# Second cross attention: two heads in a 32-row lane, weights divided on GpSimd, keys as 128 + 26

## What is computed

```python
def proj(x, W, bias):
    return (x @ W.T + bias).reshape(b, -1, NH, DK).transpose(0, 2, 1, 3)   # NH = 16, DK = 16
q, k, v = proj(X, Wq, bq), proj(ctx, Wk, bk), proj(ctx, Wv, bv)
scores = jnp.einsum('bhqd,bhkd->bhqk', q, k) / jnp.sqrt(jnp.float32(DK))
scores = jnp.where(attn_mask[:, None, :, :], jnp.float32(-1000000000.0), scores)
attn = jax.nn.softmax(scores, axis=-1)
ctx = jnp.einsum('bhqk,bhkd->bhqd', attn, v)
x = x + ctx.transpose(0, 2, 1, 3).reshape(b, -1, NH * DK) @ Wo.T + bo
```

## Time and profile before

| | |
|---|---|
| median of 3 executions | 2185.2 us (2185.1 to 2185.9) |
| the profiled execution | 2184.0 us, span of its instructions 2182.1 us |
| busy in the span | PE 1971.4, DVE 1548.9, ACT 1235.0, POOL 917.2 us |
| mean granted clock of PE | 0.949 of full |
| stage E | from about 1500 us to 1734 us of the span |

### The profile page before, as it was taken

The page is one execution under the profiler, slowest core; times in us unless marked ns, Lnnn a source line. Parts: engine busy times, 40 slices in busy tenths (PEclk is TensorE's granted clock), DMA queues, the critical chain, the costliest instruction groups (busy, mean ns, idle before and its releaser), DMA issues.

```text
span 2182.1 us, 63983 instructions
## 1 busy us (share of the span) xinstructions
PE 1971.4 (90%) x25992; PEld 1664.2 (76%) x25992; DVE 1548.9 (71%) x4226; ACT 1235.0 (57%) x3476; POOL 917.2 (42%) x1122
## 2 busy tenths in 40 slices
PE   5899999999998999987999679898998889999997
PEld 4688888888876788876899557676666678888886
DVE  5876777677754576656676268776788679889887
ACT  4655446545522677751555357776875336656564
POOL 2443344244132555541688644441111015556654
PEclk9899999999999999998999889999997789999999
DMA  4201001000100300011353400000000027767664
GB/s 125 63 12 41 32 12 41 31 25 29 53 26 2 129 21 21 17 53 61 102 122 88 98 13 2 2 3 32 3 2 24 27 93 197 180 169 180 174 155 92
DMA packets 101453, 139.31 MB, mean 64 GB/s; under 512 B 33252, under 2 KB 79848, under 8 KB 99752
## 3 DMA queue, kind: packets, MB, share of 16 engines
q1 hardware_dynamic: 80040, 104.93, 15.5%
q0 software_dynamic: 21120, 30.29, 8.0%
HBM read 111.86 MB, written 23.33 MB: 62 GB/s over the span
## 4 chain that ended last, share of the span: by engine, by line
PE 44%; DVE 13%; issue 6%; ACT 3%; POOL 3%; DMA 2%; POOLq 0%; SPq 0%; DVEq 0%; ACTq 0%
PE bank L3294 9%; PE bank L2060 8%; PE bank L1613 4%; DVE f_Y L3478 2%; PE bank L2487 2%; PE bank L1669 1%; PE bank L2878 1%; PE bank L2474 1%; PE bank L2508 1%; PE bank L2931 1%; PE bank L1709 1%; PE bank L2901 1%; PE bank L2493 1%; PE bank L2524 1%; PE bank L2915 1%
## 5 line engine op out<-in xcount | busy, mean ns | idle before, releaser
L1113 DVE SCALAR_TENSOR_TENSOR a_acc<-a_praw,a_convw,a_acc 128x256 f32<-128x256 f32 x345 | 198.5, 582 | 9.5 <-ACT a_acc L1262 1.2
L3572 POOL DMA_INDIRECT out<-f_Y,f_id x78 | 131.6, 1687 | 141.0 <-DVE f_Y L3478 95.8
L1200 DVE COPY_PREDICATED wa<-masks,bank 128x512 f32<-128x512 uint8 x128 | 93.4, 732 | 94.6 <-PE bank L1014 94.3
L3294 PE MATMUL bank<-f_exT,f_wp 128*128 128x256 f32 (+1 forms) x816 | 149.8, 332 | 5.1 <-DVE f_wp L613 2.7
L913 PE MATMUL bank<-XT,wa 128*128 128x256 f32 x512 | 146.8, 416 | 0.0
L3294 PEld LDWEIGHTS bank<-f_exT,f_wp 128*128 128x128 f32 x816 | 122.8, 192 | 19.8 <-DVE f_Hp L3459 3.3
L311 POOL TENSOR_SCALAR rs<-mv 128x2 f32<-128x2 f32 x42 | 11.9, 283 | 283.1 <-DVE mv L292 282.0
L1338 ACT ACTIVATE wa<-bank 128x256 f32<-128x256 f32 x160 | 59.2, 384 | 109.7 <-PE bank L1000 108.8
L2661 ACT ACTIVATE d_P<-d_P,d_mx 128x256 f32<-128x256 f32 (+1 forms) x256 | 106.8, 484 | 16.4 <-DVE d_mx L2588 14.4
L1000 PE MATMUL bank<-wa 64*64 64x64 f32 x2560 | 105.0, 225 | 12.1 <-DVE wa L1200 6.9
L1000 PEld LDWEIGHTS bank<-wa 64*64 64x64 f32 x2560 | 86.7, 136 | 34.6 <-issue 14.0
(11 more groups left out here) (503 smaller groups left out, 6055.8 us busy)
## 6 DMA issues: line engine op xcount, KB each, us to landing
wa<-in_f_w SPq DMA_DIRECT2D x114, 384.0 KB
wa<-in_c_w SPq DMA_DIRECT2D x64, 256.0 KB, 3.3
wb<-grown SPq DMA_DIRECT2D x4, 1536.0 KB, 7.2
a_KQg<-grown SPq DMA_DIRECT2D x4, 1536.0 KB, 7.4
a_E<-decays SPq DMA_DIRECT2D x16, 256.0 KB, 3.8
X<-in_x SPq DMA_DIRECT2D x4, 512.0 KB, 5.6
wa<-in_a_wqkv SPq DMA_DIRECT2D x1, 2048.0 KB, 8.7
summed<-X SPq DMA_DIRECT2D x8, 256.0 KB, 2.1
```

The lines of the kernel that those rows point to most:

```text
L1113: i = v.e.scalar_tensor_tensor(A_, praw[:, c, :, j:j + BT_], convw[:, c, j:j + 1], A_, ALU.mult, ALU.add)
L1200: i = v.e.copy_predicated(xx[c % 2], masks[:, l].unsqueeze(2).broadcast_to([P, 2, H, R]), b.ap.rearrange("p (w h r) -> p w h r", w=2, h=H))
L3294: i = t.e.matmul(out_, lhsT[x], rhs[y], start=n == 0 and first, stop=n == 2 and last_, skip_group_check=True)
L3572: g.e.indirect_dma_start(out_rows, bass.IndirectOffsetOnAxis(ido[t % 4][:, m:m + 1], 0), Y[t % 2][:, m, :], None, bounds_check=B * T - 1, ...
```

## The change

- Keys and queries are packed: a lane of 32 partitions now holds two heads. The keys of a lane lie in `KT` twice, once with the second head's rows set to zero and once with the first's, side by side as 308 columns (DVE writes them, with a factor of 0 or 1 by partition, `const("lane")`). One matmul then gives both heads' scores: 4 of 308 columns for 8 of 154. The projections of queries and keys have 2 column blocks for 4.
- The exponentials also add up their rows (`accum_out`). Two new steps for each half group follow: `invert` (DVE, reciprocals of four sums) and `scale` (POOL, divides the weights of four heads: 104 elements of the last 26 keys into `Pr`, and 512 of the first 128 keys in place).
- A head's 128 first keys are one slot of 128 x 128; the last 26 keys of the eight heads lie in lanes of 32 in two more slots. That makes 10 slots and 20 transposes: 8 in the first `turn`, 12 in the second. They come two groups behind the scores, and the products three.
- `mix` has 8 products over 128 keys and 8 over 26 (`VR`, four at once on the diagonal of the array). Two heads of a lane add into one block of 32 rows, since `V` and `VR` are zero in the other head's columns. The result already lies as the output product wants it, so ACT copies it straight into `AOT`; `across` and `flip` are gone.
- `Pm` has three buffers of eight heads for two, and POOL clears `Pr`, `VR` and `V` at the start. The position lists have a tile of their own (`lane`) instead of `Q[0]`. DVE has the key evictions that ACT had, and 16 small additions for `VR`.

```diff
@@ stage_e: tiles @@
-            MT, NPB = AH * 32 // P, 8
-            KT = t_("KT", [P, MT, B * S2])
-            V = t_("V", [HALF, B, 2, AH, 32])
-            OT = [t_(f"OT{i}", [P, 2, P]) for i in range(2)]
-            Pm = [t_(f"P{i}", [P, 2, S2]) for i in range(NPB)]
-            PT = [t_(f"PT{i}", [HALF, 2, 2, 2, P]) for i in range(NPB // 2)]
+            KT = t_("KT", [P, KD, B, 2, S2])
+            V = t_("V", [P, B, AH, 2 * AD])
+            VR = t_("VR", [P, B, KD, 2, 2 * AD])
+            lanes = [t_("lane", [P, 16 * P])[:, :], xn[:, :, :, :].rearrange("p i m c -> p (i m c)")]
+            Pm = [t_(f"P{i}", [P, 8, S2]) for i in range(3)]
+            Pr = [t_(f"Pr{i}", [P, 2, 4, SLOT]) for i in range(3)]
+            PT = [t_(f"PT{i}", [P, 10, P]) for i in range(2)]
@@ stage_e: order @@
-            order += [("norm", "E", NT // 2 - 1), ("value", 0, 0), ("value", 0, 1), ("ln", "E", NT // 2 - 1)]
-            order += [("value", 1, 0), ("value", 1, 1)]
+            order += [("norm", "E", NT // 2 - 1), ("value", 0), ("rest", 0), ("ln", "E", NT // 2 - 1)]
+            order += [("value", 1), ("rest", 1)]
...
-                turn = [("turn", g - 1, h) for h in range(2)] if 0 <= g - 1 < G else []
+                turn = [("turn", g - 2, h) for h in range(2)] if 0 <= g - 2 < G else []
...
-                order += turn[0:1] + [("mix", g - 2)] * (0 <= g - 2 < G)
-                order += scores + exps[0:1] + [("flip", n)] * (g % 2 == 0 and 0 <= n < NT) + turn[1:2] + exps[1:4]
+                order += scores[0:2] + [("mix", g - 3)] * (0 <= g - 3 < G)
+                for what in ("invert", "scale"):
+                    order += [(what, g - 1, 1)] * (0 <= g - 1 < G)
+                order += turn[0:1] + scores[2:3] + exps[0:1] + turn[1:2] + scores[3:4] + exps[1:2]
+                for what in ("invert", "scale"):
+                    order += [(what, g, 0)] * (g < G)
...
-                order += [("across", g - 2)] * (0 <= g - 2 < G)
...
-                    order += [("query", g // 8 + 1, g % 8 // 2)]
+                elif g // 8 + 1 < NT // 4 and g % 8 in (3, 5):
+                    order += [("query", g // 8 + 1, g % 8 // 4)]
+                order += exps[2:4]
@@ stage_e, PE @@
+                        t.wait_ge(scaled.sem, scaled.at[g, h])
+                        for i in range(4 + 2 * h):
+                            for half, rows_ in enumerate(halves):
+                                part = Pm[g % 3][rows_, 4 * h + i, 0:P] if i < 4 else (
+                                    Pr[g % 3][rows_, i - 4, :, :].rearrange("p r n -> p (r n)"))
+                                y = t.e.transpose(by_slot(h, at[s + (half,)].ap)[:, i, :], part, ident[rows_, rows_],
+                                                  tile_position=(rows_.start, 0))
...
+                        for q in range(4):
+                            t.e.matmul(b.ap[:, 0:2 * S2], Q[n // 4 % 2][lane(q), m, n % 4 * P:(n % 4 + 1) * P],
+                                       KT[lane(q), m, n // TB, :, :].rearrange("p i n -> p (i n)"), start=True, stop=True,
+                                       tile_position=(SLOT * q, 0), skip_group_check=True).then_inc(b.filled, 1)
...
                         for j in range(2):
+                            for r in range(4):
+                                t.e.matmul(b.ap[lane(r), 0:P], V[:, bb, 8 * m + of(r, j), :], PT[g % 2][:, of(r, j), :],
+                                           start=j == 0, stop=False, tile_position=(0, SLOT * r), skip_group_check=True)
                         for j in range(2):
+                            for r in range(4):
+                                i = t.e.matmul(b.ap[lane(r), 0:P], VR[lane(r), bb, m, j, :], PT[g % 2][lane(r), 8 + j, :],
+                                               start=False, stop=j == 1, tile_position=(SLOT * r, SLOT * r), skip_group_check=True)
@@ stage_e, DVE @@
+                    elif what == "key":
+                        for i in range(2):
+                            y = v.e.tensor_scalar(KT[:, m, :, i, :], b.ap[:, 0:B * S2].rearrange("p (b n) -> p b n", b=B),
+                                                  bk[:, m:m + 1], const("lane")[:, i:i + 1], ALU.add, ALU.mult)
...
+                        v.wait_ge(weighted.sem, weighted.at[g, 2 * h + 1])
+                        v.e.reciprocal(rec[:, g % 3, four], total[:, g % 3, four]).then_inc(inverted.sem, 1)
@@ stage_e, ACT @@
-                            i = c.e.activation(part, part, ACT.Exp, bias=mx[:, of(g, r), j:j + 1], scale=-1.0)
+                            i = c.e.activation(part, part, ACT.Exp, bias=shift, scale=-1.0, accum_out=total[:, g % 3, k:k + 1])
@@ stage_e, POOL @@
+                        g.wait_ge(inverted.sem, inverted.at[i, h])
+                        g.e.tensor_tensor(Pr[i % 3][:, :, 2 * h:2 * h + 2, 0:REST].rearrange("p j r n -> p r j n"),
+                                          p_[:, :, P:S2].rearrange("p (r j) n -> p r j n", j=2),
+                                          bc(r_.rearrange("p (r j) -> p r j", j=2), REST), ALU.mult)
+                        g.e.tensor_tensor(p_[:, :, 0:P], p_[:, :, 0:P], bc(r_, P), ALU.mult).then_inc(scaled.sem, 1)
```

More of the change, by code:

```diff
@@ L3019, in scalar @@
                     what, b = s[0], at.get(s)
[L3020 to L3024 removed]
+                    if what == "ln":
                         ln_act(c, s)
```

208 lines of the change are left out of this document (96 added, 112 removed).

## The result

The change is faster by less than half of what was forecast: median 2170.9 us (2166.4 to 2173.0, five executions) against 2185.9 (2185.1 to 2192.0) for the kernel before on the same chip, a ratio of 0.9933 with the interval 0.9914 to 0.9953. That is about 15 us, where 32 were forecast: the interval lies clear of 1, and the gain is under 1%. The profiled execution took 2167.4 us against 2184.0 before.

A forecast was written before the change was run, and what follows sets the result against it. PE was taken as the bound until group 21, then DVE with PE behind. Preparation -2, groups 0 to 20 -21, groups 21 to 30 -9 and tail 0 summed to -32: median 2153 us, range 2133 to 2173.

The forecast's parts named there:

- preparation: Before group 0, 1500 to 1515: PE sheds key and query blocks, DVE evicts keys; -2 us (-5 to +1).
- groups 0 to 20: Second stretch: filling, 18 groups of 4.4 us, plus 2 for splitting, 91 for 112; -21 us (-28 to -10).
- groups 21 to 30: Routing stretch: DVE's work -5, its idle time brings this to -7, port price +3; -9 us (-18 to -3).
- tail: After the routing stretch: DVE -1, one more group of transposes and products +1; 0 us (-3 to +3).
- plus 2 for the weight splitting from group 14 on: Within groups 0 to 20: weight splitting adds 2 us to the filling and 18 groups of 4.4 us.
- The clock rival: First 21 groups: PE's clock falls to 1.2 GHz, 6.4 us a group, +19 in 18 groups, about 2200 us; chance 0.06.
- DVE's extra work: Per group: norm, statistics, output on DVE and a query on ACT; about half show, 0.4 to 0.5 us above 3.9.
- one group more of transposes and products stands behind the inverse list: +1: Tail: an additional group of PE work follows the inverse list, adding 1 us against DVE's -1.
- GpSimd at the pace: Rival: GpSimd, 80% busy, sets a group of 5.0 us; 2169 us in all; chance 0.18.
- all waits hide: Rival: group period 4.0 us, routing stretch -15; 2141 us in all; chance 0.14.
- The port's price: Routing stretch: twelve norms and some twenty routing operations on DVE collide with GpSimd, 0.1 us each; +3 us.
- The gain reached the end: Against the rival that the last feed-forward, starting on routing and weights, returns the gain: 2183 to 2186 us; chance 0.05.

The follow-up runs named there:

- e3: Changed kernel with each output product made twice, the second into unused columns, adding PE work to every second group; 2177.1 us, 0.9966 of the kernel before.
- e16: Kernel before the change, with DVE's splitting half a group later and the last position-list steps later; 2180.5 us, 0.9987 of the kernel before.
- e5: Changed kernel with DVE's part of the stage F splitting half a group later, ACT's part unmoved; 2167.0 us, 0.9910 of the kernel before.
- e17: Repeat of e11: changed kernel with DVE's splitting half a group later and the last position-list steps later; 2153.4 us, 0.9885 of the kernel before.
- e12: The changed kernel measured once more, unedited; 2167.8 us, 0.9918 of the kernel before.
- e7: Changed kernel with the last three position-list steps later, PE's 24 products behind the last output product; 2167.6 us, 0.9926 of the kernel before.
- e13: Changed kernel with three extra, never-read PE matmuls behind the products in groups 15, 17 and 19; 2166.4 us, 0.9934 of the kernel before.
- e11: Changed kernel with DVE's splitting half a group later and the last position-list steps later; 2156.1 us, 0.9883 of the kernel before.
- e2: Changed kernel with GpSimd's large division cut to 26 of the 128 keys of each head; 2168.4 us, 0.9920 of the kernel before.
- e15: e11 with the splitting's subtractions moved from DVE to GpSimd; 2162.1 us, 0.9909 of the kernel before.

## Why the prediction was right or wrong

**What bounds, and what takes over: right in the main.** The undisturbed period is 4.56 us where 4.4 (4.2 to 4.7) was forecast, ACT is the busiest (96%), the chain passes between PE, DVE and ACT, and in the routing stretch groups take 7.1 us (forecast 7.0) with DVE busy 59.4 of 71.2, 83% for the 85 put there. PE, though, showed 95% busy, not under 85. Part of that is waiting: a block of scores that takes 0.80 us by itself shows as 1.84 + 0.78 us where its banks come free one by one (1541.88). Part of it is work: PE holds 21.3 of the 36.9 us of the chain, and what e3 added to it came out at 60%. It is no longer the bound alone, and no run shows it as free.

**The sum, term by term** (profiled execution):

| term | forecast | measured |
|---|---|---|
| preparation | -2 | -3.2 |
| groups 0 to 20 | -21 | -7.6 |
| groups 21 to 30 | -9 | -8.4 |
| tail | 0 | +5.1 |
| stage E | -32 | -14.1 |

**The step that failed is "plus 2 for the weight splitting from group 14 on".** Groups 12 to 21 were to take 9 x 4.4 + 2 = 41.6 us and took 51.2. The price was taken as if the splitting were work in a row of work. It is a wait of one engine for another that has just become the slower one, at the head of the queue that PE's scores depend on. In the kernel before it was shorter, and the backlog of PE, which held the chain there, covered about half of it (1.5 us of wait, 0.8 us gained in e16); with the backlog gone it showed in full, and the clock fell twice beside it. Late by half a group, the stretch takes 44.3 us (e5, e17). Of the 9.6 us missed this is 7. The rest of the 13.4 us missed in groups 0 to 20 is 2.6 in the filling and 1.3 in groups 4 to 12.

**The clock rival was given 0.06 and as a whole slowdown; it came in part.** It was thought of as a slowdown that holds or not over the whole stretch. At 4.56 us a group the full clock held through groups 4 to 12 in the changed kernel's profile; in e12, e7 and e13, the same code up to there, it fell for 3.4 or 6.8 us. It cost some 2.7 us for 6.8 at 1.2 GHz (e7 and e13 against the changed kernel). In groups 12 to 21 the two falls went with DVE's waits (e5, e11 and e17: without them none). They do not go by a gap's length: e5 and e17 have the gap of 0.89 us too and keep the clock, and e13 lost it with 0.34 and 0.31. The Trainium skill ("TensorE: Matmul & The Clock Gate", Part 4) says that transposes do not count as activity the way other matmuls do, by which fewer transposes should not have hurt. The clock fell twice between groups 12 and 21 where it had not before; no run here separates transposes from other matmuls.

**Smaller misses in the same stretch:** the scores 0.78 us for 0.50, the products 1.14 for 1.01, ACT's exponential 0.41 for 0.38. The 0.50 was misread. It is the time from the first weight load of a block to the next line's weight loads; the matmuls of that block in stage B take 0.80 us (from 850.30). And the four matmuls of 308 columns overlap fully, but one alone takes as long as all four, and the loop waits for the last bank:

```profile
1543.87 0.78 PE L2904 MATMUL bank<-e_KT,e_Q 32*128 32x308 f32 x2 [0.16 <-DVE e_mx L3010]
1548.20 0.80 PE L2904 MATMUL bank<-e_KT,e_Q 32*128 32x308 f32 x8
```

(A matmul leaves two rows: the first line is one matmul, the second four.) The period is longer than forecast by 0.16 us, 1.3 us over groups 4 to 12. These terms add up to 0.4 in the loop and 0.25 on ACT, and how much of the forecast's 0.4 to 0.5 for DVE's extra work showed was not measured. Filling took 16.9 us to group 4 for 14.3, at a mean clock of 0.70 (first row of the table by stretch), with 10.2 us at 1.2 GHz from 1513.0 on where the kernel before had none; that was not tried.

**The tail, 0 (-3 to +3), was +5.** The term "one group more of transposes and products stands behind the inverse list: +1" had the mechanism and the wrong size. This is the second step that failed: it was priced at the full clock and beside other work; it stands in the chain alone at 1.2 GHz, 1711.35 to 1713.5 for products alone. With the lists' last products behind it the tail is 24.0 to 27.7.

**GpSimd at the pace (0.18), all waits hide (0.14): neither.** The first had 2169 us, and 2170.9 was measured. That is a coincidence: e2 excludes it, its period was to be 5.0 and was 4.56, and transposes waited for GpSimd 1.4 us in the 88 us from 1525 on, 0.4 at most at a time. The port's price, +3, was about right: against e2 the norms lost 2.3 us of DVE's time and nine routing operations 3.3. The Trainium skill ("SBUF — State Buffer", who interferes with whom) has the second of two colliding operations stand still until the first is done; e15's 2.31 us for 0.28 beside GpSimd's subtraction agrees with it.

**The gain reached the end**, within the 8 us by which stage F varies from profile to profile.

## What to carry to other kernels

When a change takes the bound off an engine, go through every place where another engine waits for a third inside the freed stretch, and price it at its full length: the old bound's backlog hid it. Moving the waiting half of the pair half a period later gave 7 us in its stretch here, and in e11 and e17 cost nothing elsewhere in the stage. A deeper pipeline costs its extra stage once at the end, at the clock that holds there; see what may go behind it. Two bounds that lie within a few per cent of each other (here ACT and the loop) make each experiment on one of them look as if it were none.
